# Q of an attention as seven block products in place of eight, and a new order of its head pairs

## The reference, cut to what matters

```
h   = rmsnorm(layernorm(x)) * ln_weight            (8 x 128 rows, 512 columns)
q   = h   @ w_q.T      k = ctx @ w_k.T      v = ctx @ w_v.T      (4096 columns each)
s   = q_h @ k_h.T + position_bias_h, masked         (per batch and head, 128 x 128)
o   = softmax(s) @ v_h
out = o @ w_out.T,     x + tanh(gate) * (layernorm(x) + out)  in the end
```

## Time and profile before

| what | us |
|---|---|
| median of three runs | 1681.8 |
| the profiled execution | 1683.32 |
| its span | 1681.2 |
| TensorE busy | 1613.6 (96%) |
| VectorE, ScalarE, GpSimd busy | 917.2, 743.0, 371.4 |
| first scores of pair 0 | at 57.44 |
| first scores of pair 14 | at 803.71 |
| first transposes of the first FFN | at 876.81 |

### The profile page before, as it was taken

How to read it: one execution, slowest core, us unless ns; L and a number is a source line. 1 busy time by engine, 2 the same in 40 slices (tenths; PEclk the granted TensorE clock), 3 DMA queues, 4 the chain that set the end, 5 groups by cost and what they waited for, 6 DMA issues and landing times.

```text
span 1681.2 us, 25841 instructions
## 1 busy us (share of the span) xinstructions
PE 1613.6 (96%) x9028; PEld 1286.2 (77%) x9028; DVE 917.2 (55%) x2467; ACT 743.0 (44%) x2177; POOL 371.4 (22%) x266
## 2 busy tenths in 40 slices
PE   9999999999999999999989999999999999999885
PEld 8888888888888888888865968787786787655454
DVE  5642533425335254352486666758485767455787
ACT  4542443424434344343333553636273332677732
POOL 3210211112111121121013300000002533355452
PEclk9999999999999999999999999999999999999978
DMA  5110101101111011110413000000004312000001
GB/s 185 54 42 34 57 28 50 41 16 65 41 50 41 16 65 41 50 39 17 131 56 152 14 1 12 0 12 0 1 1 161 104 50 91 14 14 14 1 1 50
DMA packets 34137, 76.09 MB, mean 45 GB/s; under 512 B 5536, under 2 KB 18336, under 8 KB 31904
## 3 DMA queue, kind: packets, MB, share of 16 engines
q1 hardware_dynamic: 34080, 75.36, 13.1%
HBM read 73.25 MB, written 2.10 MB: 45 GB/s over the span
## 4 chain that ended last, share of the span: by engine, by line
PE 72%; DVE 16%; ACT 5%; issue 3%; DVEq 2%; POOL 1%; POOLq 0%; DMA 0%; ACTq 0%; SPq 0%
PE banks L996 14%; PE banks L1006 10%; PE banks L1093 10%; PE banks L1197 9%; PE banks L1301 5%; PE banks L1273 3%; PE banks L1064 3%; DVE sA L1671 3%; PE banks L1079 2%; ACT sA L686 2%; PE banks L1411 2%; PE banks L1425 2%; PE banks L1432 2%; PE banks L1404 1%; PE banks L1071 1%
## 5 line engine op out<-in xcount | busy, mean ns | idle before, releaser
L1694 DVE TENSOR_TENSOR x_res<-banks,x_res 128x512 f32<-128x512 f32 x120 | 82.8, 691 | 207.7 <-PE banks L1093 207.4
L996 PE MATMUL banks<-cT,w_k 128*128 128x512 f32 x720 | 179.8, 398 | 0.0
L1006 PE MATMUL banks<-w_v,cT 128*128 128x512 f32 x768 | 179.8, 392 | 0.0
L996 PE MATMUL banks<-xT,w_q 128*128 128x512 f32 x720 | 175.4, 396 | 0.0
L686 ACT ACTIVATE sA<-sA,nmA 128x128 f32<-128x128 f32 x256 | 99.3, 390 | 166.4 <-DVE nmA L1671 165.5
L1093 PE MATMUL banks<-w_o,atT 128*128 128x512 f32 x720 | 170.4, 393 | 2.1 <-DVE x_res L1694 2.0
L1006 PEld LDWEIGHTS banks<-w_v,cT 128*128 128x128 f32 x768 | 142.7, 188 | 28.9
L1093 PEld LDWEIGHTS banks<-w_o,atT 128*128 128x128 f32 x720 | 134.0, 188 | 31.3 <-DVE x_res L1694 2.4
L996 PEld LDWEIGHTS banks<-xT,w_q 128*128 128x128 f32 x720 | 131.9, 188 | 25.5
L996 PEld LDWEIGHTS banks<-cT,w_k 128*128 128x128 f32 x720 | 130.8, 188 | 25.2
L1678 DVE TENSOR_SCALAR rsA<-smA 128x4 f32<-128x4 f32 x64 | 15.7, 246 | 185.5 <-ACT sA L686 185.5
(11 more groups left out here) (245 smaller groups left out, 3236.2 us busy)
## 6 DMA issues: line engine op xcount, KB each, us to landing
w_raw_k<-in_w0k SPq DMA_DIRECT2D x16, 512.0 KB, 3.2
w_raw_v<-in_w0v SPq DMA_DIRECT2D x8, 1024.0 KB, 7.1
w_raw_q<-in_w0q SPq DMA_DIRECT2D x15, 512.0 KB, 3.3
w_raw_o<-in_w0o SPq DMA_DIRECT2D x15, 512.0 KB, 3.3
cTp<-in_ctxT SPq DMA_DIRECT2D x12, 512.0 KB, 4.3
wq_raw<-in_wq SPq DMA_DIRECT2D x1, 3072.0 KB, 11.1
wo<-in_wo SPq DMA_DIRECT2D x1, 3072.0 KB, 20.9
kT<-in_ctxT SPq DMA_DIRECT2D x4, 512.0 KB, 6.3
```

The costliest lines, as they stand in the source:

```text
L996: mm = pe.matmul(dst, w[l][:, c, h * P:(h + 1) * P], t[r][:, c, half * 512:(half + 1) * 512], start=n == 0, stop=n == 3 * DC - 1)
L1006: mm = pe.matmul(dst, cT[l][:, c, b * P:(b + 1) * P], wv_[r][:, c, :], start=n == 0, stop=n == 3 * DC - 1)
L1694: dve.tensor_tensor(x_res[:, b, :], bank(6 + b % 2), x_res[:, b, :], ALU.add).then_inc(S("o_added"), 1)
```

## The change

- Q of a pair is a 256 x 512 matrix times 512 x 1024 columns. Both are cut into 2 x 2 blocks (heads by feature halves, feature halves by token halves), and the four blocks of Q are formed from seven block products with sums ahead and behind (`PRODUCTS`, `query_unit`): 7 x 2 chunks x 3 passes = 42 matmuls of 128 x 512 instead of 48. Ahead, VectorE forms four sums of weight blocks (`weight_sums`) and, once in the kernel, four sums of row blocks (`rows_sums`). Weights and rows so have seven blocks in place of four, and their high and low parts are made for all seven; for the rows GpSimd makes the low part of three blocks. Behind, VectorE adds the products 1 to 6 from the banks into `qT` (`query_sum`); ScalarE stores product 0.
- Score groups are by token halves: g = 0, 1 are heads 0, 1 of the first half. The first half's output products (4 batches) are done in the pair itself, those of the second half in the next pair. `qT`, `kT` and the attended rows `atT` are held once, not twice.
- The order of each engine is new. Pair 0 is written out, 1 to 12 are a loop, 13 to 15 are written out. Pair 14 adds its outputs through the gate, and the residual is prepared there (`begin_sum`).
- The loads follow the new order; the last pair's output weights go through the K buffer; the FFN's first weights are issued when all products of pair 14 are done. Ahead of the loop the rows are transposed in pairs of batches k and k + 4.

The diff, cut to its core:

```diff
-QK_UNITS, V_UNITS = 8, NB
-UNITS_0 = QK_UNITS + V_UNITS
-UNITS_2 = 2 * QK_UNITS + V_UNITS
-UNITS_ALL = UNITS_0 + NHP // 2 * QK_UNITS + (NHP // 2 - 1) * (QK_UNITS + V_UNITS)
+Q_UNITS, K_UNITS, V_UNITS = 7, 4, NB
+STEP_UNITS, STEP_COPIES = K_UNITS + Q_UNITS, K_UNITS + 1
+UNITS_0, COPIES_0 = STEP_UNITS + V_UNITS, STEP_COPIES + V_UNITS
+UNITS_2, COPIES_2 = 2 * STEP_UNITS + V_UNITS, 2 * STEP_COPIES + V_UNITS
+UNITS_ALL = UNITS_0 + (NHP - 1) * STEP_UNITS + (NHP // 2 - 1) * V_UNITS
+HT = NB * P // 2
+
+
+
+W11, W12, W22, WS3, WS1, WS2, WS4 = range(7)
...
+PRODUCTS = ((W11, X11), (WS2, XT2), (W12, X21), (WS1, XT1), (WS3, XT3), (WS4, X22), (W22, XT4))
...
+def steps(eng, body):
+    body(step_at(0))
+    with eng.Fori(0, NHP // 2 - 2) as it:
+        body(Step(2 * it + 1, 1, it + 1, UNITS_0 + STEP_UNITS + UNITS_2 * it, COPIES_0 + STEP_COPIES + COPIES_2 * it))
+        body(Step(2 * it + 2, 0, it + 2, UNITS_0 + UNITS_2 + UNITS_2 * it, COPIES_0 + COPIES_2 + COPIES_2 * it))
+    for p in range(NHP - 3, NHP):
+        body(step_at(p))
...
+                if par == 0:
+                    sp.wait_ge(S("pj"), units)
+                    if is_step(p, NHP - 2):
+                        sp.dma_start(x_raw[:], x_dram).then_inc(S("x_again"), 16)
+                    else:
+                        load("v", A["w0v"][turn])
+                if not is_step(p, 0):
+                    sp.wait_ge(S("o_done"), NB * p + 1)
+                    load("o", A["w0o"][p])
+                sp.wait_ge(S("pj"), units + K_UNITS)
+                if is_step(p, NHP - 2):
+                    load("k", A["w0o"][NHP - 1])
+                    return
+                load("k", A["w0k"][p + 2])
+                load_bias(p + 2, par)
+                sp.wait_ge(S("pj"), units + STEP_UNITS)
                 load("q", A["w0q"][p + 2])
-                load_bias(p + 2, par)
-                sp.wait_ge(S("pj"), base + 8)
-                load("k", A["w0k"][p + 2])
...
+            split("q", 0)
+            for k in range(NPAIR):
+                t = slice(k * P, (k + 1) * P)
+                pool.wait_ge(S("x_hi"), k + 1)
+                pool.tensor_tensor(xT[1][:, XT1:, :, t], stage[k % 2][:, XT1:], xT[0][:, XT1:, :, t].bitcast(F32),
+                                   ALU.subtract).then_inc(S("x_split"), 1)
...
+                split("q", p + 1)
+                split("o", p)
+                split("k", p + 2)
+                if par == 0 and not is_step(p, NHP - 2):
+                    split("v", turn)
...
+                keys(0)
                 store_pT(p, 0)
+                store_at(p, 0)
+                if not last:
+                    round_q(p + 1)
+                keys(1)
+                store_pT(p, 1)
+                if last:
+                    store_at(p, 1)
                 exps(p, 2)
-                store_at(p, 0)
-                store_pT(p, 1)
-                store_at(p, 1)
+                keys(2)
+                if not last:
+                    store_at(p, 1)
+                exps(p, 3)
+                keys(3)
+                if not last:
+                    store_half(q_at(0, 1), unit_bank(K_UNITS), units + K_UNITS + 1)
+                    round_w("o", p)
+                    round_w("k", p + 2)
+                if par == 0 and not is_step(p, NHP - 2):
+                    round_w("v", turn)
                 store_pT(p, 2)
-                exps(p, 3)
                 store_at(p, 2)
-                round_w("q", NHP - 1)
                 store_pT(p, 3)
                 store_at(p, 3)
-
-            with act.Fori(0, (NHP - 2) // 2) as it:
-                head_pair(2 * it, 0, UNITS_0 + UNITS_2 * it, it + 1, True)
...
+            def query_unit(m, dst):
+                w, x = PRODUCTS[m]
+                for c in range(2):
+                    for n, (l, r) in enumerate(PASSES):
+                        mm = pe.matmul(dst, wq_[l][:, w, c, :], xT[r][:, x, c, :], start=c == 0 and n == 0,
+                                       stop=c == 1 and n == len(PASSES) - 1)
+                mm.then_inc(S("pj"), 1)
+
+            def queries_of(p, m, copies, dst):
+                if m == 0:
+                    pe.wait_ge(S("wq_lo"), p + 1)
+                if m < 3:
+                    pe.wait_ge(S("pj_out"), copies + m)
+                else:
+                    pe.wait_ge(S("q_out"), Q_UNITS * p + (1, 2, 3, 5)[m - 3])
+                query_unit(m, dst)
...
+                if not first:
+                    out(p - 1, 4)
+                    out(p - 1, 5)
+                keys(0)
+                if not first:
+                    out(p - 1, 6)
+                turn_probs(0)
+                scores(2)
+                if not first:
+                    out(p - 1, 7)
                 attend(0)
-                proj_unit(3)
-                scores(2)
-                turn(1)
-                proj_unit(4)
+                keys(1)
+                turn_probs(1)
+                scores(3)
+                keys(2)
                 attend(1)
-                proj_unit(5)
-                scores(3)
-                turn(2)
-                proj_unit(6)
+                keys(3)
+                for m in range(5):
+                    queries(m)
+                for b in range(4):
+                    if b == 3:
+                        turn_probs(2)
+                    out(p, b)
                 attend(2)
-                proj_unit(7)
-                turn(3)
+                turn_probs(3)
+                queries(5)
+                attend(3)
+                queries(6)
...
+            def weight_sums(n):
+                w = wq_block
+                dve.wait_ge(S("wq_ld"), 16 * (n + 1))
+                dve.tensor_tensor(w[:, WS1], w[:, WS3], w[:, W22], ALU.add)
+                dve.drain()
+                dve.tensor_tensor(w[:, WS3], w[:, W11], w[:, WS3], ALU.subtract)
+                dve.tensor_tensor(w[:, WS2], w[:, WS1], w[:, W11], ALU.subtract)
+                dve.drain()
+                dve.tensor_tensor(w[:, WS4], w[:, W12], w[:, WS2], ALU.subtract).then_inc(S("q_sum"), 1)
...
+            def rows_sums(k):
+                x = stage[k % 2]
+                if k >= 2:
+                    dve.wait_ge(S("x_split"), 2 * k - 1)
+                for j in range(2):
+                    dve.wait_ge(S("xr_used"), 2 * k + j + 1)
+                    dve.tensor_tensor(x[:, 2 - 2 * j:4 - 2 * j].rearrange("p s c t -> p (s c) t"),
+                                      bank(4 + j).rearrange("p (c t) -> p c t", c=DC),
+                                      ln_w[:].unsqueeze(2).to_broadcast([P, DC, P]), ALU.mult).then_inc(S("xw_ready"), 1)
+                dve.drain()
+                dve.tensor_tensor(x[:, XT1], x[:, XT3], x[:, X11], ALU.subtract)
+                dve.drain()
+                dve.tensor_tensor(x[:, XT3], x[:, X22], x[:, XT3], ALU.subtract)
+                dve.tensor_tensor(x[:, XT2], x[:, X22], x[:, XT1], ALU.subtract)
...
+            def rows_low(k):
+                t = slice(k * P, (k + 1) * P)
+                dve.wait_ge(S("x_hi"), k + 1)
+                dve.tensor_tensor(xT[1][:, 0:XT1, :, t], stage[k % 2][:, 0:XT1], xT[0][:, 0:XT1, :, t].bitcast(F32),
                                   ALU.subtract).then_inc(S("x_split"), 1)
...
+            def query_sum(first, copies, m, n):
+
+                dve.drain()
+                dve.wait_ge(S("pj"), first + m + 1)
+                if m == 1:
+                    dve.wait_ge(S("pj_out"), copies + 1)
+                    e = dve.tensor_tensor(q_at(1, 1), q_at(0, 1), bank(n), ALU.add)
+                if m == 2:
+                    e = dve.tensor_tensor(q_at(0, 1), q_at(0, 1), bank(n), ALU.add)
+                if m == 3:
+                    e = dve.tensor_tensor(q_at(0, 0), q_at(1, 1), bank(n), ALU.add)
+                if m == 4:
+                    dve.tensor_tensor(q_at(1, 1), q_at(1, 1), bank(n), ALU.add).then_inc(S("q_out"), 1)
+                    e = dve.tensor_tensor(q_at(1, 0), q_at(0, 0), bank(n), ALU.add)
+                if m == 5:
+                    e = dve.tensor_tensor(q_at(0, 0), q_at(0, 0), bank(n), ALU.add)
+                if m == 6:
+                    e = dve.tensor_tensor(q_at(1, 1), q_at(1, 1), bank(n), ALU.subtract)
+                e.then_inc(S("q_out"), 1)
...
+                if not first:
+                    add_out(p - 1, 4)
+                norm(0)
+                if not first:
+                    add_out(p - 1, 5)
+                norm(1)
+                weight_sums(p + 1)
+                scores(2)
+                if not first:
+                    add_out(p - 1, 6)
+                rest(0)
+                if not first:
+                    add_out(p - 1, 7)
+                if gated:
 ...
+                scores(3)
+                rest(1)
+                norm(2)
+                norm(3)
+                for m in range(1, 5):
+                    query_sums(m)
+                for b in range(4):
+                    if gated:
```

(19 more changed lines are left out.)

559 lines of the change are left out of this document (246 added, 313 removed).

## The result

The changed kernel takes 1662.44 us (median of 4 runs, 1661.42 to 1663.99), the kernel before beside it 1681.97 (4 runs). The ratio is 0.9885, with a 95% interval of 0.9864 to 0.9906. The forecast was 1660.5 us. The profiled execution of after took 1662.29 us (forecast 1662.1), its span is 1660.3. In a later comparison on another chip the same kernel took 1665.91 against 1681.95, ratio 0.9903 [0.9886, 0.9921]; where the 3.5 us between the two come from is shown under `again`.

What follows compares the result with a forecast made beforehand. TensorE, busy 96% of the span, was taken as the bound. Pairs 0 to 13 -34.5, start +10.5, pairs 14 and 15 +2.8 sum to -21.2 us, median 1660.5; 66% for 1655 to 1667, 8 in 10 for 1651 to 1673.

Steps and rivals of the forecast that it cites:

- part 1: Q of each head pair: seven products replace eight, 42 matmuls for 48, 1.36 us less TensorE time in each of 16 pairs.
- part 2: New engine order in a pair: even pair 40.24 us, odd 62.0, two pairs saving 4.4 us.
- the term -34.5: Forecast sum for pairs 0 to 13, in us; ends -36 with no wait, -12 if tight places cost 1.5 a pair.
- The lock: GpSimd's wide subtractions hold VectorE's SBUF-only passes; in the loop score group 3 is held to 18.6, at cost 0.
- The tightest place: Product 1 of Q waiting for ScalarE's store of the last keys: 0.5 us to spare.
- part 3: Start before pair 0's first scores: row preparation nearly in series, locks and slow clock; Q ends at 68.0, +10.5 us.
- part 4: Pairs 14 and 15: 42.4 and 33.5 us, together 75.9, +2.8 us (0 to +6).
- Nothing changes behind the attention: The stretch behind 876.81 us in the old trace keeps its time: change 0.
- 1 (tight place): Rival, 14%: exponentials 3 come 1 to 1.5 us later, each pair waits 0.5 to 1; about 12 us less gain, 1672.
- 3 (Q weight chain): Rival, 6% together with the fourth: product 0 waits for weight sums, rounding and low part; slower than before, 1693 us.
- 2: Rival, 14%: the start is cheaper, with locks shared kindly and TensorE's stalls half; -27 to -28 us, 1654.
- 4: Rival, 6% together with the third: seven products take no less TensorE time because two-row-block operands stream slower.

Runs made afterwards that it cites:

- again: The changed kernel with no edit, measured a second time on another chip: 1665.91 us, ratio 0.9903 to the kernel before.
- eighth: Changed kernel with the last of Q's seven products computed twice in every pair: 1686.2 us, ratio 1.0021 to the kernel before.
- twice: Changed kernel with seven extra GpSimd subtractions of 256 columns ahead of each low part of the Q weights: 1693.27 us, ratio 1.0059 to the kernel before.
- late1: Changed kernel with one extra ScalarE pass of 512 columns per pair before the store of the last keys: 1667.73 us, ratio 0.9905 to the kernel before.
- late2: Changed kernel with two extra ScalarE passes of 1024 columns per pair before the store of the last keys: 1682.52 us, ratio 1.0002 to the kernel before.
- lows: Changed kernel with VectorE making the rows' low parts of all seven blocks and GpSimd none: 1660.16 us, ratio 0.9856 to the kernel before.
- gated: Changed kernel with pair 14's four residual passes moved behind score group 3: 1664.43 us, ratio 0.9887 to the kernel before.
- resid: Changed kernel with the eight residual scaling passes placed between pair 0's product sums, not ahead of them: 1667.45 us, ratio 0.9906 to the kernel before.
- best: Changed kernel with the edits of resid, lows and gated together: 1656.65 us, ratio 0.9844 to the kernel before.
- best2: As best, but five scaling passes ahead of the sums and one behind each of products 1 to 3: 1658.07 us, ratio 0.9856 to the kernel before.

## Why the prediction was right or wrong, point by point

**Seven products (part 1): right.** 1.35 us a product, by eighth.

**The order in a pair (part 2): right, 0.2 us a pair short.** The forecast was 40.24 and 62.0, the trace has 40.40 and 62.20. The walk holds nearly instruction by instruction: product 0 was put 22.4 us behind the first scores and began 22.69 behind them; output 0 was put at 29.2 and came at 29.49. The forecast took 2.72 us for every unit of twelve, but one that follows a small group takes 2.82: 173.50 - 170.68 here, and in the old trace 178.14 - 175.32, from the earlier trace rows and this row of it:

```profile
178.14 1.05 PE L1064 MATMUL banks<-kT,qT 128*128 128x128 f32 x8
```

So the unit at 190.80 in the earlier trace rows ended 0.1 us later than counted, and the wait that went away was 0.73 and not 0.83 us. The pair is 42.58 - 40.40 = 2.18 us shorter, so with the six matmuls' 1.36 some 0.09 are left for the one island less, where the forecast put 0.15. The odd pair is 1.86 shorter for a forecast of 2.06, which the prediction gives without its parts. Over pairs 1 to 13 that is 6 x 0.16 + 7 x 0.2 = 2.4 of the 2.6 us by which the term -34.5 was too large. The chain of the Q weights, GpSimd, ScalarE and VectorE in the pair shown above:

```profile
183.66 4.05 POOL L516 TENSOR_TENSOR w_q<-w_raw_q,w_q 128x1792 fp32r<-128x1792 f32 x1 [46.21 <-ACT w_q L706]
...
191.87 0.60 ACT L696 ACTIVATE kT<-banks 128x512 f32<-128x512 f32 x1 [0.60 <-PE banks L1023]
...
186.31 1.54 DVE L1769 CUSTOM_DVE_ANT_0 sA<-sA,madd 128x128 f32<-128x128 f32 x1
...
194.68 0.69 DVE L1721 TENSOR_TENSOR qT<-qT,banks 128x512 f32<-128x512 f32 x1 [1.66 <-PE banks L1031]
```

The low part is ready at 187.71, 4.0 us ahead of product 0 (forecast 3.8; `twice` found 3.8). The lock hits score group 3, whose pass takes 1.54 in place of 0.29, and costs TensorE nothing, as forecast. The tightest place was named rightly, but under-counted: the store ends at 192.47, 0.56 us ahead of product 1 (193.03), as forecast, and ScalarE is idle for another 0.60 ahead of it, which the forecast's own numbers had in part (22.2 to 22.6) and did not count as slack for the exponentials. Together 1.16, which late1 and late2 bear out.

**The start (part 3): the mechanism was right, the size 2.3 us too small.** The stretch in after, VectorE, TensorE and GpSimd:

```profile
36.37 1.96 DVE L1692 TENSOR_TENSOR stage_o<-stage_o 128x256 f32<-128x256 f32 x1
...
42.48 1.29 DVE L1685 TENSOR_TENSOR stage_q<-banks,ln_w 128x512 f32<-128x512 f32 x2 [2.51 <-POOL xT L528]
...
49.29 1.29 DVE L1685 TENSOR_TENSOR stage_o<-banks,ln_w 128x512 f32<-128x512 f32 x2 [2.54 <-POOL xT L528]
...
52.00 0.42 DVE L1694 TENSOR_TENSOR stage_o<-stage_o 128x256 f32<-128x256 f32 x1
...
57.56 5.81 DVE L1712 TENSOR_SCALAR x_res<-x_res,mv,rstd 128x512 f32<-128x512 f32 x8
...
43.31 1.94 PE L1072 MATMUL banks<-ident,xr 128*128 128x128 f32 x8 [3.88 <-DVE stage_q L1685]
44.91 10.40 PE L1048 MATMUL banks<-w_v,cT 128*128 128x512 f32 x36
57.14 4.37 PE L1031 MATMUL banks<-xT,w_q 128*128 128x512 f32 x18 [1.83 <-POOL xT L528]
64.31 6.05 PE L1031 MATMUL banks<-xT,w_q 128*128 128x512 f32 x24 [2.79 <-DVE qT L1721]
70.20 1.95 PE L1137 MATMUL banks<-kT,qT 128*128 128x128 f32 x16
76.28 0.66 PE L1144 MATMUL banks<-ident,sA 128*128 128x128 f32 x4 [1.40 <-DVE sA L1781]
...
54.24 2.85 POOL L528 TENSOR_TENSOR xT<-stage_o,xT 128x768 fp32r<-128x768 f32 x1 [4.99 <-ACT xT L719]
```

The term that was mis-sized is the work of one row pair on VectorE, two multiplications and four block sums: the forecast has 1.2 + 1.5 = 2.7 us, the trace 3.1, with 0.42 us for a block sum that was put at 0.35 (the four of the first pair run from 30.99 to 34.12). Four such pairs in series are 1.6 us, and the scaling passes ahead of them ended at 31.1 and not at 30.3. So the sums of the last pair ended at 52.4 and not at 50.0, the low parts came at 57.1 and not at 54.8, and everything behind is later by as much (product 3 at 64.31 for 61.7, first scores at 70.20 for 68.0). The two waits for GpSimd, 5.05 us together, are in the forecast's text; beyond the 0.4 us a row pair they were priced rightly, from one pair's sums to the next 6.8 us for 6.4. Product 3's wait, 2.79 (forecast 2.7), and its cause, mask and scaling passes ahead of the sum of product 1, were right. The idle ahead of product 0 is 1.83 us and not about 4, since TensorE ended the values near 55.3 and not at 50.8; that costs nothing, as product 0 waits for the low parts. Of the clock, the place was right and the charge partly wrong: behind the idle before 43.31 the granted clock was 0.50, and the 36 matmuls lost 10.40 - 8.45 = 2.0 us, hidden under the wait for the low parts; behind the 2.79 it stayed at 1.00, so the 0.8 us that the forecast put there was not paid; in `again` and in lows it was, with 1.3 and 1.6 us. These are windows of after (columns as above):

```profile
43.00:47.00 4.00, 3.69 (x13) 3.33 (x14) 3.51 (x7) 1.35 (x1) 0.00 (x0) 0.50 0.00 0
...
64.00:71.00 7.00, 6.67 (x32) 5.34 (x33) 4.20 (x7) 0.00 (x0) 0.00 (x0) 1.00 0.00 0
```

The start lost 12.8 us, just inside the 13 that the forecast named as its bound; in `again` it lost 13.7, beyond it.

**Pairs 14 and 15 (part 4): too dear by 2.1 us.** Pair 14 took 41.41 (forecast 42.4), pair 15 32.35 (33.5). VectorE and TensorE there:

```profile
784.58 1.95 PE L1137 MATMUL banks<-kT,qT 128*128 128x128 f32 x16
...
799.10 6.53 DVE L1794 SCALAR_TENSOR_TENSOR x_res<-x_res,gates,x_raw 128x512 f32<-128x512 f32 x4 [0.18 <-issue]
...
809.51 5.74 PE L1031 MATMUL banks<-xT,w_q 128*128 128x512 f32 x24 [0.72 <-ACT kT L696]
...
825.99 1.95 PE L1137 MATMUL banks<-kT,qT 128*128 128x128 f32 x16
...
858.34 1.04 PE L1228 MATMUL banks<-ident,xn 128*128 128x128 f32 x8
```

The four passes were held as forecast (6.53 us for four of 0.7), but product 1 waited 0.72 us and not 1.6, and the second wait did not come: the slack of the tightest place, again under-counted by half a microsecond or more. `gated` confirms the cause, with pair 14 at 40.40. In pair 15 the 1.3 us for a slow clock was not paid in after; in `again` it was, and its pair took 33.97: that much of this term's error is luck too.

**Nothing changes behind the attention: right for the code, wrong for the time**, by the clock as far as the traces show, -2.4 us. Together with the -2.1 of part 4 it cancels the errors of the start and of the pairs. Without that luck, `again` gives 1665.9, 5 us above the forecast and inside its range.

**Rivals.** 1 (tight place) and 3 (Q weight chain) didn't come about, and late2 and twice show both with the points from which they decide; 2 had the wrong sign, the start was dearer than forecast and not cheaper; 4 falls by eighth.

## What to carry to other kernels

Where TensorE has no idle time, work taken from it counts in full and the new chains beside it cost nothing up to a slack that can be counted from the old trace to some tenths; spend the care on the part that runs once, where latencies stand in series. Look at what each wait really protects: a threshold one step too high cost 3.1 us here. When a wait is taken away, see who is next on the same engine's list, and judge an edit by the stretch it touches, since two measurements of the same kernel lay 3.5 us apart, most of it where the granted clock differed.

## What the runs showed of the hardware

- A slow stretch of TensorE that a later wait hides comes into the open when that wait is taken away: in resid, best and best2 the 42 matmuls took 11.6 to 11.7 us for 9.5, behind idle times of 2.83, 1.93 and 1.92 us.
- After the same 1.50 us of TensorE idle the granted clock was 1.00 or 0.50, in executions of one kernel; 24 matmuls took 5.7 to 8.6 us.
- GpSimd's hold takes small VectorE passes too: a 128 x 4 maximum with a constant took 2.79 us in `twice`, to GpSimd's end at 558.74. And it goes both ways: GpSimd's last 768-column subtraction took 2.85 us beside VectorE's 1.23 us pass, which began 0.04 us ahead of it, where the others took 1.80 to 2.11.
- The Trainium skill ("GPSIMD Engine Reference", section "Key points") names VectorE instructions in a two-port mode or with two SBUF inputs as those that contend. The block sums with two SBUF inputs agree (1.24 for 0.43 us). The 128 x 4 pass has one SBUF input, and no run here shows in which mode it ran.
- One float32 addition of 128 x 256 in SBUF takes 0.42 us, where half of the 128 x 512 one from PSUM would be 0.35.
